# Unit 0's query in two halves and two banks, its first scores ahead of the context's values, and two loads on ScalarE's queue

## The reference

```
x1  = x + tanh(g_xattn) * (attention(layernorm(x), ctx, mask) @ w_o + b_o)
out = x1 + tanh(g_ffn) * ffn(layernorm(x1))
attention: q = layernorm(x) @ w_q + b_q        16 heads of 16
           k = ctx @ w_k + b_k, v = ctx @ w_v + b_v
           softmax(q k^T / 4, masked) @ v
ffn: softmax gate over 4 experts, the best 2 kept and renormed; each expert and
     one shared expert is  (silu(x g) * (x u)) @ d,  inner width 688
x: (4, 1024, 256) fp32    ctx: (4, 77, 256)    mask: (4, 1, 1024, 77) int32
```

## Time and profile before

| | |
|---|---|
| median of 3 executions | 868.1 us (867.94 to 869.85) |
| the profiled execution | 869.38 us |
| its span (first to last instruction) | 867.7 us |
| granted clock of TensorE, mean | 0.991 of full speed |
| PE busy | 837.4 us (97%) |
| DVE, ACT, POOL busy | 585.3, 522.0, 468.8 us |

### The profile page before, as it was taken

One profiled execution on the slowest core, in us unless ns is written; L12 is line 12 of the kernel. 1 busy time (PEld: TensorE's weight loads), 2 busy tenths in 40 slices (PEclk: granted clock), 3 DMA queues, 4 the chain that ended last, 5 costly groups with the idle time before them and its releaser, 6 DMA issues.

```text
span 867.7 us, 19215 instructions
## 1 busy us (share of the span) xinstructions
PE 837.4 (97%) x6183; PEld 733.5 (85%) x6184; DVE 585.3 (67%) x1214; ACT 522.0 (60%) x1846; POOL 468.8 (54%) x562
## 2 busy tenths in 40 slices
PE   8788899999999999999999999999999999999994
PEld 6567788888888799999988888888888888889994
DVE  6889889898888657976565666655665655454442
ACT  3989999999999635646565544445445454323231
POOL 5678678697575443666631444444444424364442
PEclk9899999999999999999999999999999999999998
DMA  7124323232222232323351444443444432232221
GB/s 222 41 79 122 117 68 98 85 106 83 76 90 63 75 109 71 119 91 113 102 153 39 76 75 71 69 65 64 69 68 68 73 50 38 31 49 42 36 42 19
DMA packets 104761, 67.84 MB, mean 78 GB/s; under 512 B 63514, under 2 KB 93055, under 8 KB 104671
## 3 DMA queue, kind: packets, MB, share of 16 engines
q1 hardware_dynamic: 90743, 48.93, 20.0%
q0 software_dynamic: 12864, 17.57, 12.6%
q10 hardware_dynamic: 1064, 0.21, 0.1%
HBM read 34.78 MB, written 25.82 MB: 70 GB/s over the span
## 4 chain that ended last, share of the span: by engine, by line
PE 86%; ACT 5%; DVE 3%; issue 2%; DMA 2%; POOL 0%; SPq 0%; DVEq 0%; ACTq 0%; POOLq 0%
PE p_s L680 23%; PE p_f L697 12%; PE p_f L2852 9%; PE p_s L347 7%; PE p_f L2897 4%; PE p_s L2852 4%; PE p_t L2782 3%; PE p_s L2763 3%; ACT prob L1564 3%; PE p_t L358 3%; PE p_m L2797 3%; PE p_m L2744 3%; PE p_m L2809 3%; PE p_s L2897 2%; PE p_s L2955 1%
## 5 line engine op out<-in xcount | busy, mean ns | idle before, releaser
L1564 ACT ACTIVATE prob<-p_s,negmax 128x77 f32<-128x77 f32 x512 | 161.7, 376 | 7.8 <-DVE negmax L2112 7.7
L1564 ACT ACTIVATION_READ_ACCUMULATOR prob<-p_s,negmax 128x1 f32 x512 | 129.9, 258 | 0.0
L537 POOL DMA_INDIRECT big_xin<-xn_scratch,slot_id x52 | 52.2, 1004 | 125.2 <-DMA big_placed<-big_xin 87.8
L581 ACT ACTIVATE big_sil<-p_s 128x512 f32<-128x512 f32 (+1 forms) x78 | 46.5, 596 | 115.7 <-PE p_s L680 102.2
L680 PE MATMUL p_s<-big_fxT_hi,big_w_hi 128*128 128x512 f32 (+1 forms) x286 | 112.8, 395 | 0.1
L680 PE MATMUL p_s<-big_fxT_lo,big_w_hi 128*128 128x512 f32 (+1 forms) x286 | 112.9, 395 | 0.0
L680 PE MATMUL p_s<-big_fxT_hi,big_w_lo 128*128 128x512 f32 (+1 forms) x286 | 112.2, 392 | 0.0
L1174 POOL TENSOR_TENSOR prob<-prob,rinv 128x616 f32<-128x616 f32 x64 | 78.9, 1237 | 58.6 <-DVE rinv L2119 58.6
L545 POOL DMA_INDIRECT out_rows<-big_yout,slot_id x52 | 85.9, 1652 | 43.8 <-DVE big_yout L643 28.2
L626 DVE TENSOR_TENSOR big_hid<-p_s,big_sil 128x512 f32<-128x512 f32 (+1 forms) x78 | 54.0, 692 | 76.8 <-ACT big_sil L581 72.0
L697 PE MATMUL p_f<-wd_hi,big_hT_hi 128*128 (+1 forms) x312 | 85.5, 280 | 0.0
(11 more groups left out here) (348 smaller groups left out, 2539.7 us busy)
## 6 DMA issues: line engine op xcount, KB each, us to landing
big_placed<-big_xin SPq DMA_DIRECT2D x176, 32.0 KB
xr<-in_x SPq DMA_DIRECT2D x16, 256.0 KB, 2.8
x_scratch<-xr SPq DMA_DIRECT2D x16, 256.0 KB, 2.4
xn_scratch<-xn SPq DMA_DIRECT2D x16, 256.0 KB, 2.1
xt_scratch<-xnT SPq DMA_DIRECT2D x16, 256.0 KB, 3.2
xin<-xt_scratch SPq DMA_DIRECT2D x16, 256.0 KB, 3.4
x1in<-x_scratch SPq DMA_DIRECT2D x16, 256.0 KB, 3.3
out_rows<-syout SPq DMA_DIRECT2D x16, 256.0 KB, 2.2
```

The lines of the kernel that those rows point to most:

```text
L537: pool.indirect_dma_start(xin[:, t, :], None, v["xn_d"], bass.IndirectOffsetOnAxis(slot_id[:, column(j, t)], 0)).then_inc(s_rows, 16)
L1564: last = act.activation(prob[n % 2][t][:, m * PW + h * SK:m * PW + (h + 1) * SK], p_s[:, 2 * t + h // 4, col:col + SK], ACT.Exp, bias=negm ...
```

## The change

Unit 0's query is made in two banks: half m = 0 stays in `p_m`, half m = 1 goes to `p_f[1]`. Each half has its own count in `s_q`, `s_qhi` and `s_qlo`, so that unit 0 counts to 2 and all later waits go through `queries(n) = n + 2`. `scores(0, 0)` and `scores(0, 1)` need half 0 only. PE makes them right behind `q_T(0)`, ahead of the keys of the other three batches, the gate's transposes and the context's values. The second half of the values waits for `p_f[1]`, that is for the low part of query half 1. DVE takes `key_hi(0)` and the low part of query half 0, then both `half_max` of these quarters, and only then `key_hi(1)`, query half 1, `rest_of_start`, `half_max(0, 2)` and the context's values. ACT does `exps(0, 0)` and `exps(0, 1)` in a row and keeps its other steps behind them; `w_hi(1)` and `w_hi(2)` come behind `exps(0, 3)`. The loads of the context and of `w_q` leave SP's list and stand first in ACT's, ahead of the six short loads.

```diff
+        def queries(n):
+            return n + 2
+        def q_bank(n, m):
+            return p_f[1][:, 0:UT * P] if n == 0 and m == 1 else p_m[:, m * UT * P:(m + 1) * UT * P]
 # SP
             load_x(0)
-            sp.dma_start(ctx_sb[:, :, :], v["ctx_in"].rearrange("b k d -> k b d")).then_inc(s_ctx, 16)
             sp.dma_start(wk[:, :, :], v["w_k"].rearrange("(c p) d -> p c d", p=P)).then_inc(s_wk, 16)
             load_mask(0)
-            sp.dma_start(wq[:, :, :], v["w_q"].rearrange("(c p) d -> p c d", p=P)).then_inc(s_wq, 16)
 # ACT
             def q_hi(n):
-                act.wait_ge(s_q, n + 1)
                 wait(act, s_S, 4 * (n - 1))
                 for m in range(KC):
+                    if n == 0 or m == 0:
+                        act.wait_ge(s_q, m + 1 if n == 0 else queries(n))
+                    last = act.activation(qT[0][:, n % 2, m, :], q_bank(n, m), ACT.Identity, bias=bq[:, m:m + 1])
+                    if n == 0 and m == 0:
+                        last.then_inc(s_qhi, 1)
                 last.then_inc(s_qhi, 1)
+            act.dma_start(ctx_sb[:, :, :], v["ctx_in"].rearrange("b k d -> k b d")).then_inc(s_ctx, 16)
+            act.dma_start(wq[:, :, :], v["w_q"].rearrange("(c p) d -> p c d", p=P)).then_inc(s_wq, 16)
             act.dma_start(bk[:, :], ...)
...
                 exps(0, 0)
+                exps(0, 1)
                 xT_copy(1)
                 other_keys_hi()
-                exps(0, 1)
+                exps(0, 2)
                 q_hi(1)
                 w_hi(0)
-                exps(0, 2)
+                exps(0, 3)
                 w_hi(1)
                 w_hi(2)
-                exps(0, 3)
 # DVE
             dve.wait_ge(s_own, 3)
-            for m in range(KC):
-                key_hi(m)
-            q_lo(0)
+            key_hi(0)
+            dve.wait_ge(s_qhi, 1)
+            q_half_lo(0, 0).then_inc(s_qlo, 1)
             stats_1(1)
...
                 half_max(0, 0)
+                half_max(0, 1)
+                key_hi(1)
+                dve.wait_ge(s_qhi, queries(0))
+                q_half_lo(0, 1).then_inc(s_qlo, 1)
                 rest_of_start()
+                half_max(0, 2)
                 context_values(0)
                 context_values(1)
-                half_max(0, 1)
+                recip(0, 0)
                 no_sight(1)
                 stats_1(2)
-                half_max(0, 2)
-                recip(0, 0)
+                half_max(0, 3)
                 q_lo(1)
                 recip(0, 1)
                 w_lo(0)
-                half_max(0, 3)
                 w_lo(1)
 # PE
             def scores(n, j):
-                if j == 0:
-                    pe.wait_ge(s_qlo, n + 1)
+                if n == 0 and j == 0:
+                    pe.wait_ge(s_qlo, 1)
+                elif j == 0 or (n == 0 and j == 2):
+                    pe.wait_ge(s_qlo, queries(n))
...
             pe.wait_ge(s_wq, 16)
+            pe.wait_ge(s_ctxT, 1 + KC)
             q_T(0)
-            pe.wait_ge(s_ctxT, 1 + KC)
+            scores(0, 0)
+            scores(0, 1)
             keys_of(1, B, p_t)
...
-                scores(0, 0)
                 values_of_context(0)
-                values_of_context(1)
-                scores(0, 1)
                 x_T(1)
                 scores(0, 2)
+                pe.wait_ge(s_qlo, queries(0))
+                values_of_context(1)
                 q_T(1)
+                scores(0, 3)
                 w_T(0)
-                scores(0, 3)
                 w_T(1)
                 w_T(2)
```

More of the change, by code:

```diff
@@ L1543, in xT_copy @@
                 act.wait_ge(s_xT, n + 1)
-                wait(act, s_q, n)
+                wait(act, s_q, queries(n - 1) if n > 0 else 0)
                 act.activation(xT[:, :, :], cols(p_m[:, :]), ACT.Copy).then_inc(s_xTc, 1)
             def q_hi(n):
-                act.wait_ge(s_q, n + 1)
                 wait(act, s_S, 4 * (n - 1))
                 for m in range(KC):
-                    last = act.activation(qT[0][:, n % 2, m, :], p_m[:, m * UT * P:(m + 1) * UT * P], ACT.Identity,
-                                          bias=bq[:, m:m + 1])
+                    if n == 0 or m == 0:
[3 more added lines that the diff above has]
+                        last.then_inc(s_qhi, 1)
                 last.then_inc(s_qhi, 1)
@@ L2085, in stats_2, with q_half_lo @@
                 stats(n, slot, 1, s_bst2, s_mv2)
+            def q_half_lo(n, m):
+                return nc.vector.scalar_tensor_tensor(
+                    out=qT[1][:, n % 2, m, :], in0=q_bank(n, m), scalar=bq[:, m:m + 1], in1=qT[0][:, n % 2, m, :],
+                    op0=ALU.add, op1=ALU.subtract)
             def q_lo(n):
-                dve.wait_ge(s_qhi, n + 1)
-                for m in range(KC):
[L2090 to L2093, removed]
+                dve.wait_ge(s_qhi, queries(n))
+                q_half_lo(n, 0)
+                q_half_lo(n, 1).then_inc(s_qlo, 1)
             def no_sight(n):
@@ L2732, in x_T @@
                 wait(pe, s_x1, n - 2)
-                wait(pe, s_qlo, n)
+                wait(pe, s_qlo, queries(n - 1) if n > 0 else 0)
                 for k in range(KC):
@@ L2743, in q_T @@
                     for k in range(KC):
-                        last = nc.tensor.matmul(p_m[:, m * UT * P:(m + 1) * UT * P], wq[:, k, m * P:(m + 1) * P],
+                        last = nc.tensor.matmul(q_bank(n, m), wq[:, k, m * P:(m + 1) * P],
                                                 xT[:, k, :], start=(k == 0), stop=(k == KC - 1))
+                    if n == 0 and m == 0:
+                        last.then_inc(s_q, 1)
                 last.then_inc(s_q, 1)
@@ L2791, in prob_v @@
                 wait(pe, s_xnc, n)
-                pe.wait_ge(s_qlo, min(n + 3, NU))
+                pe.wait_ge(s_qlo, queries(min(n + 2, NU - 1)))
                 for m in range(KC):
@@ L2816, in xn_T @@
                 pe.wait_ge(s_x1, n + 1)
-                pe.wait_ge(s_qlo, min(n + 4, NU))
+                pe.wait_ge(s_qlo, queries(min(n + 3, NU - 1)))
                 for k in range(KC):
```

## The result

The changed kernel takes 871.07 us in the median of 8 executions (869.90 to 872.06), the kernel before 868.10 (867.13 to 870.06, 8 executions): ratio 1.0028, with a 95% interval of 1.0019 to 1.0038, so 0.2% to 0.4% slower. The ratio weighs all executions and isn't that of the medians: these differ by 2.97 us, the means by 2.40. Predicted were 870.5 us.

The account below looks back on a forecast made before the run. The prediction took the early chain through `prob_v(0)`, then PE nearly without a gap from 96.69 us, as the bound. Blocks 2.4 us late made 871.8 from 869.38; the median, 1.3 below, gave 870.5 us, range 867.3 to 872.7.

Parts of the forecast that it names:

- The knot at `prob_v(0)`: PE's `prob_v(0)`, until now released by DVE's query at 42.12, would wait for SP's late blocks until 44.55: 2.4 us late.
- The biases land at 11.0, and beyond 9.25 every microsecond goes through one for one: ACT's queue: biases behind 564 KB delay `keys_T` and the key chain, putting the first maxima at 15.1.
- the case of the earliest landing: ACT's queue: lower end, 9.2, of the 9.2 to 13.2 us in which the biases were said to land.
- The sum of 870.1 for the span: Whole kernel: the profiled span of 867.7 us plus 2.4 us of delay at `prob_v(0)`, everything behind it unchanged.
- if nothing ahead moves: DVE's start: `key_hi(0)` still at 10.52, so first maxima at 13.35, a head start of 2.5 us.
- The second branch: DVE and ACT, `half_max(1, 0)` to unit 2's query: done at 43.4, 1.4 us late, hidden behind the blocks.
- The clock takes it back: Rival at PE's `prob_v(0)`: at full clock 1.68 us come back, 868.8 us; chance 0.10.
- the biases in time: Rival on ACT's queue: biases delay nothing, only the blocks are late, +0.7 us, 868.8 us; chance 0.24 (in time or nearly).

Follow-up runs that it names:

- run 5: Kernel before with six more small moves into HBM scratch ahead of SP's 24 block moves: 870.16 us, 1.0021 of before.
- run 1: Changed kernel with the blocks' moves made in 12 transfers instead of 24: 870.15 us, 1.0022 of the kernel before.
- run 3: Kernel before with only the loads of context and `w_q` moved to ACT's queue: 1.0003 of before.
- run 4: Changed kernel with the loads of context and `w_q` back on SP's queue: 871.94 us, 1.0035 of the kernel before.
- run 10: Changed kernel with 26 needless PE transposes, 8 ahead of `x_T(0)` and 18 between `w_T(1)` and `w_T(2)`: 1.0029 of the kernel before.
- run 6: Run 1's kernel with `w_hi(1)` back ahead of `exps(0, 3)` and `w_lo(2)` behind `half_max(1, 0)`: 1.0017 of the kernel before.
- run 8: Run 6's kernel with `normalise(0, 0)` ahead of `rstd1(2)`, `scores(0, 3)` ahead of `q_T(1)`, `context_values(0)` ahead of `half_max(0, 2)`: 1.0027 of the kernel before.
- run 2: Kernel before with the blocks' moves made in 12 transfers instead of 24: 1.0000 of before.
- run 12: Kernel before with 12 transfers, 16 needless PE transposes in gaps and 10 more ahead of `prob_T(0, 3)` and `prob_T(0, 4)`: 866.79 us, 0.9978 of before.
- Run 11: Run 6's kernel with the same 26 needless PE transposes as run 10: 1.0005 of the kernel before.

## Why the prediction was right, step by step

The forecast was right in sign and near in size: 2.4 us forecast, 2.97 measured by the medians and 2.40 by the means. The release by the blocks was foreseen and is in the profile. But two wrong terms cancel in the place of the first maxima, which is luck, and the branch that was called hidden is nearly as late as the blocks.

*The knot at `prob_v(0)`: right.* Values complete at 24.40 (24.4 forecast), SP's first move right behind at 24.43, release by a DMA at 44.39 (44.55). The landing that no row of before showed took 1.88 us from issue where I took 2.1. Run 5 makes the same delay in the kernel before, run 1 removes this release from the changed one. But run 1 also shows that the blocks alone don't make the loss: without them 1.0022 of 1.0028 stays. From first maxima to values: 9.23 for 9.3.

*"The biases land at 11.0, and beyond 9.25 every microsecond goes through one for one": wrong in both halves.* They landed at 9.5, near the case of the earliest landing, 9.2. The error is in what stands ahead of them: `w_q` landed at 7.0 (issued at 1.50, 5.5 to landing), where I had 9.0; from there the biases took 2.5 where I had 2.0. The rows are from after's timeline and from its DMA view (size, us to landing):

```profile
1.50 0.42 ACTq L1646 DMA_DIRECT2D wq<-in_L_xattn_w_q  x1
```

```profile
wq<-in_L_xattn_w_q ACTq DMA_DIRECT2D x1, 256.0 KB, 5.5
```

And a late `keys_T` is not what held the key chain: in run 3 it was done at 10.29, but ACT's `kT_hi` stood in its list behind the copy of `x_T(0)` until 10.72. That copy came late because `x` did, and it gave the biases a slack that I had not counted. The sum of 870.1 for the span needed 1.75 us from this term; the queue alone cost 1.0003 of before, nothing that can be told. The Trainium skill's "DMA: Bandwidth & Descriptors", Queues, rings and completion order, has the queues served by turns. The trace agrees in that `x`, with 308 KB beside it in the other queue, landed later than before (statistics at 5.45 for 4.89); no run here shows in what order the short rows went. What was wrong was my pace for the 564 KB.

*What stood in its place:* the first maxima at 15.17 (15.1 forecast) come through `x`. Its statistics start at 5.45 for 4.89 before; the chain of waits now begins with `x`'s load, 4.51 us. In all eight kernels with the context on ACT's queue they start at 5.44 to 5.69, in all six with it on SP's at 4.86 to 4.89: the context's load, now issued at the same moment as `x`, most likely shares its transfer (no run moves the context without `w_q`). PE then waits 1.32 us for `xh`, and in this profile the clock falls: `x_T(0)` took 1.11 us and half 0 of `q_T(0)` 1.87, for 0.66 and 1.10 in run 4, whose clock was full there. Run 10 fills the gap and gets 14.06. But runs 1, 6 and 8 have 13.97 to 14.03 with the changed kernel's start as it stands, so the fall is not there in every execution. Without it the first maxima come at the 13.35 of "if nothing ahead moves" and the 0.6 that `x` is late; against before's profile that is a head start of 1.8 us, against runs 2 and 12, whose `w_q` was in time, only 1.0. The prediction gave `x` of unit 1 until 14 us and no cost; in run 4, where the first maxima would have been earlier, it cost 0.84.

*The second branch: mechanism right, mis-sized.* From first maxima to `half_max(1, 0)` 18.16 for 17.7 forecast; `w_lo(1)` waited 1.39 for 1.2; query done at 43.91 for 43.4, so 1.93 late, not 1.4. It was hidden, as said, but by 0.4 us only (43.91 against the blocks' 44.30), which is why run 1 gains so little. The prediction's own terms for 17.7 add up to 17.6. The part I left out is POOL: its `prob` for `prob_T(0, 0)` comes later when DVE's part is mended (31.00 in run 6 for 29.33 before).

*"The clock takes it back": a rival I gave 0.10, and in the profiled execution it happened.* `prob_v(0)` took 1.93 us, 1.68 less than before's. What it does to the 0.28%, a ratio of many executions, no run shows directly. Before has profiles of the same start with `prob_v(0)` at 3.61 us and at 1.94 (run 2), and the spans of 29 of its executions go from 864.6 to 868.5 at mean clocks of 0.994 to 0.988. The median of that mean clock is 0.990 for both kernels, which speaks against a share of the clock as a whole, but not against a spell that falls in a worse place in one of them. I argued that a longer gap ahead of `prob_v(0)` would keep the clock low; the gap grew to 0.79 us and the clock was full. So the argument was bad, and leaving the term out of the sum was right only for the median. By the prediction's own figures this case with the biases in time is 867.1 (868.1 + 0.7 - 1.7), which the range, from 867.3 on, doesn't quite take in.

What stays open: why the clock falls behind one gap and not behind another of the same length (after's gap of 1.32 us ahead of 9.29 and run 6's of 1.33 at the same place), and how the 0.28% divides between the blocks, the second branch and the clock. Run 11 gives back most of it with the blocks' delay, the weights' order and two gaps mended at once.

## What to carry to other kernels

Find the one instruction that all early branches meet in, and measure every edit by when it ends, not by the head start at its source: here scores 0.7 us earlier ended as `prob_v(0)` starting 2.27 later, because the work pushed behind them fed a long string of small DMA issues and a second branch nearly as late. Before reordering, ask which engine's idle stretches move, and whether cheap filler work can hold TensorE's clock through the meeting point: 26 needless transposes and half the transfers took 0.22% off the kernel before, which none of the reorderings did, while in the changed kernel 26 transposes alone won nothing (run 10). And do not take a difference between two single profiles for the edit's: here the same start gave first maxima at 15.04 and at 15.86, by when one load landed. Compare the intervals, then the rows, and look for a second profile of the same code.

## What the hardware showed

- What is issued beside a first load delays it: `x` (256 KB) landed 0.6 to 0.8 us later in all eight kernels that issued 308 KB on the other queue at the same moment, and 256 KB 0.7 us behind.
- SP issued 24 moves of up to 77 rows in 18.75 us and 12 moves of twice the content in 10.34: 0.78 and 0.86 each, so this price is by transfer, hardly by its content. But six moves of 77 rows of 64 bytes from the same tile to HBM issued in 2.29 (run 5), 0.38 each, so it isn't the same for every destination.
- The same 32 matmuls took 1.93 us at 2.4 GHz and 2.88 to 3.64 with the clock down for part or all of them. Kernels with the same list for PE had it at either level (before and run 2).
- The clock that a view lists seems to miss a spell now and then: in run 5 it is 1.00 from 6 to 11 us, where the eight matmuls of the first keys took 1.83 us for 1.09 and four transposes 1.06 for 0.66, as long as at half clock (1.11 in after).
